# Attention stage of a hybrid block: ScalarE instead of VectorE copies the turned maxima of each half sequence to 16 bits

## The reference

```python
def _L0_attn_b_ref(x, W_qkv, W_q_lsr, W_k_lsr, lsr_core, W_o):   # x: 32 sequences, 256 tokens, 128 wide; 16 heads of 8
    ql = jnp.einsum('bhtd,hdr->bhtr', q, W_q_lsr)
    kl = jnp.einsum('bhsd,hdr->bhsr', k, W_k_lsr)
    scores = jnp.einsum('bhtr,bhsr->bhts', ql * lsr_core[None, :, None, :], kl) * scale
    scores = jnp.where(causal[None, None], scores, -jnp.inf)
    attn = jax.nn.softmax(scores, axis=-1)
    y = jnp.einsum('bhts,bhsd->bhtd', attn, v)
    return y.transpose(0, 2, 1, 3).reshape(b, t, d) @ W_o
```

## Time and profile before

| | us |
|---|---|
| median of 3 runs | 2333.87 (2331.89 to 2334.64) |
| profiled execution, its own time | 2342.5 |
| its span, first to last instruction | 2340.8 |
| granted PE clock over the span | 0.827 of full speed; 1.00 from 1180 to 1740 us |
| DVE busy | 1857.7 (79%) |
| PE busy | 1654.0 (71%) |
| ACT busy | 1471.0 (63%) |
| POOL busy | 1342.9 (57%) |

### The profile page before, as it was taken

The page is one execution under the profiler, slowest core; times in us unless marked ns, Lnnn a source line. Parts: engine busy times, 40 slices in busy tenths (PEclk is TensorE's granted clock), DMA queues, the critical chain, the costliest instruction groups (busy, mean ns, idle before and its releaser), DMA issues. The chain is left out here.

```text
span 2340.8 us, 52167 instructions
## 1 busy us (share of the span) xinstructions
PE 1654.0 (71%) x16780; PEld 1352.2 (58%) x16780; DVE 1857.7 (79%) x4943; ACT 1471.0 (63%) x3849; POOL 1342.9 (57%) x1496
## 2 busy tenths in 40 slices
PE   4676675766657369995689999999986459998000
PEld 2444454454546158884488888888875338887000
DVE  6999999999978957776689999999975867776221
ACT  5666676766743647774388888888883457776000
POOL 3545555555540045554399999999971035553774
PEclk8778787777865679998699999999995579999555
DMA  1000001010034013333122222222214013333232
GB/s 29 14 14 22 20 14 28 14 27 14 19 104 140 1 48 81 81 80 58 39 57 57 57 59 59 59 57 57 57 28 129 23 27 81 81 81 67 74 80 57
DMA packets 188967, 122.59 MB, mean 52 GB/s; under 512 B 24320, under 2 KB 177824, under 8 KB 188704
## 3 DMA queue, kind: packets, MB, share of 16 engines
q1 hardware_dynamic: 154016, 75.18, 11.6%
q0 software_dynamic: 17408, 35.69, 6.9%
q10 hardware_dynamic: 17280, 8.40, 1.2%
HBM read 66.22 MB, written 44.04 MB: 47 GB/s over the span
## 5 line engine op out<-in xcount | busy, mean ns | idle before, releaser
L1044 POOL DMA_INDIRECT ffn_xs<-normed,ffn_tokeni x288 | 273.1, 948 | 460.1 <-DVE posi L1420 260.7
L1877 POOL TENSOR_TENSOR att_pl<-att_p,att_ph 128x384 f16<-128x384 f32 x512 | 455.3, 918 | 56.3 <-ACT att_ph L2098 48.6
L323 POOL TENSOR_TENSOR sq<-states,qS 128x256 f32<-128x256 f32 x256 | 250.9, 980 | 304.3 <-DVE states L733 303.3
L543 ACT ACTIVATE decayed<-states,alpha 128x64 f32<-128x64 f32 x1024 | 272.3, 336 | 177.6 <-DVE states L733 175.7
L379 PE MATMUL bank<-sq,ident 128*128 128x128 f32 x1024 | 249.9, 415 | 93.4 <-POOL sq L323 93.4
L2206 DVE TENSOR_REDUCE att_mx<-bank 128x3 f32<-128x384 f32 x512 | 279.9, 552 | 41.0 <-PE bank L1934 36.8
L1251 ACT ACTIVATE ffn_h<-bank,b_cols 128x256 f32<-128x256 f32 x576 | 226.4, 475 | 127.7 <-PE bank L1139 117.4
L379 PEld LDWEIGHTS bank<-sq,ident 128*128 128x128 f32 x1024 | 220.0, 240 | 128.9 <-POOL sq L323 100.7
L2095 ACT ACTIVATE att_p<-bank 128x384 f32<-128x384 f32 x512 | 252.2, 493 | 58.9 <-PE bank L1971 55.5
L2098 ACT ACTIVATE att_ph<-bank 128x384 f16<-128x384 f32 x512 | 253.0, 494 | 0.0
L1152 PE MATMUL bank<-w_h,ffn_hh 128*128 x1152 | 225.6, 223 | 14.9 <-DVE ffn_hl L1439 4.5
(11 more groups left out here) (336 smaller groups left out, 5085.5 us busy)
## 6 DMA issues: line engine op xcount, KB each, us to landing
slots<-ffn_ys SPq DMA_DIRECT2D x144, 128.0 KB
ffn_x_all<-x SPq DMA_DIRECT2D x16, 512.0 KB, 4.8
normed<-ffn_xn ACTq DMA_DIRECT2D x32, 256.0 KB, 2.3
att_qz<-att_qp SPq DMA_DIRECT2D x256, 32.0 KB
ffn_xs<-normed,ffn_tokeni POOLq DMA_INDIRECT x288
xin<-in_x SPq DMA_DIRECT2D x64, 64.0 KB, 2.0
xres<-in_x SPq DMA_DIRECT2D x64, 64.0 KB, 2.0
x<-x SPq DMA_DIRECT2D x64, 64.0 KB, 1.8
```

The costliest lines, as they stand in the source:

```text
L323: nc.gpsimd.tensor_tensor(sq[:, t, :].rearrange("p (h i j) -> p h i j", h=HL, i=D), states[:, t, :].rearrange("p (h i j) -> p h i j", h=HL ...
L543: ins = nc.scalar.activation(decayed[:, 64 * h:64 * h + 64], states[:, (t - 1) % TC, 64 * h:64 * h + 64], ACT.Copy, scale=alpha[p][:, t, h ...
L1044: pool.indirect_dma_start(xs[j % AHEAD][:, r, :], None, A["normed"], bass.IndirectOffsetOnAxis(ap=tokeni[:, BR * j + r:BR * j + r + 1], ax ...
L1877: nc.gpsimd.tensor_tensor(pl[:, h % RP, :], p32[:, h % RP, :], ph[:, h % RP, :], ALU.subtract).then_inc(low_done, 1)
```

## The change

The copy of the turned maxima to `mst` (L2237) leaves DVE and goes to ACT as an activation with the function Copy, in a new function `maxima_rows`; 64 copies of 128x512 elements move. On ACT it stands behind the exponentials of head 3 (second half) and of head 11 (first half). A new semaphore `maxi_act` counts the copies; SP and PE wait for it where they waited for DVE's count. For the first sequence the copy stands between two small pieces of the layer norm of sequence 2.

```diff
-MAXI_SECOND_AT = dict(larger1=0, high1=0, low1=0, rows1=3)
-MAXI_FIRST_AT = dict(larger0=9, high0=9, low0=9, rows0=11)
+MAXI_SECOND_AT = dict(larger1=0, high1=0, low1=0)
+MAXI_FIRST_AT = dict(larger0=9, high0=9, low0=9)
...
+MAXI_ACT_AT = {3: 1, 11: 0}
...
+        def rows_written(eng, b, n):
+            eng.wait_ge(maxi_act, 2 * b + n + 1)
...
             def place(i, p, n):
                 b = NBUF * i + p
-                sp.wait_ge(maxi_dve, at(MAXI, b, f"rows{n}"))
+                rows_written(sp, b, n)
...
                 elif name == "q23":
                     if not under(b, 2):
-                        pe.wait_ge(maxi_dve, at(MAXI, b - 2, "rows1"))
+                        rows_written(pe, b - 2, 1)
...
+            def maxima_rows(i, p, n):
+                b = NBUF * i + p
+                act.wait_ge(maxi_pe, 2 * b + n + 1)
+                if not under(b, 1):
+                    ii, pp = sooner(i, p, 1)
+                    act.wait_ge(m_in[n][pp], 16 * HL * (ii + 1))
+                a(mst[n][:, :, :].rearrange("p g t -> p (g t)"), ps_x[n][:, :], ACT.Copy).then_inc(maxi_act, 1)
...
-            for name in FRONT_ACT:
+            for name in FRONT_ACT[:-1]:
                 front(name, 0, 2)
+            maxima_rows(0, 0, 0)
+            front(FRONT_ACT[-1], 0, 2)
...
                 for h in range(H):
                     exps(i, p, h)
+                    if h in MAXI_ACT_AT and (MAXI_ACT_AT[h] or later(i, p, 1)):
+                        maxima_rows(*((i, p) if MAXI_ACT_AT[h] else later(i, p, 1)), MAXI_ACT_AT[h])
...
-                else:
-                    dve.wait_ge(maxi_pe, 2 * b + n + 1)
-                    if not under(b, 1):
-                        ii, pp = sooner(i, p, 1)
-                        dve.wait_ge(m_in[n][pp], 16 * HL * (ii + 1))
-                    ins = v.tensor_copy(mst[n][:, :, :].rearrange("p g t -> p (g t)"), ps_x[n][:, :])
```

More of the change, by code:

```diff
@@ L1648 @@
 FRONT_DVE_HELD = [n for n in FRONT_DVE if n not in ("xn0", "xn1", "x_low")] + ["scale", "xn0", "x_low"]
-MAXI = ["maxima0", "larger0", "high0", "rows0", "maxima1", "larger1", "high1", "rows1"]
+MAXI = ["maxima0", "larger0", "high0", "maxima1", "larger1", "high1"]
+MAXI_ACT_AT = {3: 1, 11: 0}
 NBUF = 4
@@ L1700, in attention @@
         (ready, cleared, front_dve, front_act, front_pe, proj_pe, proj_act, proj_dve, maxi_dve, maxi_pe, tail_dve, tail_pe,
-         tail_act, s_ps, max_done, st_ps, exp_done, high_done, low_done, pv_done) = (
+         tail_act, s_ps, max_done, st_ps, exp_done, high_done, low_done, pv_done, maxi_act) = (
             sem(n) for n in ("ready", "cleared", "front_dve", "front_act", "front_pe", "proj_pe", "proj_act", "proj_dve",
                              "maxi_dve", "maxi_pe", "tail_dve", "tail_pe", "tail_act", "s_in_psum", "max_done",
-                             "st_in_psum", "exp_done", "high_done", "low_done", "pv_done"))
+                             "st_in_psum", "exp_done", "high_done", "low_done", "pv_done", "maxi_act"))
         ps_s, ps_st, ps_y, ps_x = bank[0:2], bank[2:4], bank[4:6], bank[6:8]
@@ L1892, in front @@
                 if not under(b, 2):
-                    pe.wait_ge(maxi_dve, at(MAXI, b - 2, "rows0"))
+                    rows_written(pe, b - 2, 0)
                 for k in range(TB):
@@ L1949, in turn_max @@
                 else:
-                    pe.wait_ge(maxi_dve, at(MAXI, b - 1, "rows1"))
+                    rows_written(pe, b - 1, 1)
                 for s in range(2):
@@ L1995, in tail_turn @@
                 elif later(i, p, 1):
-                    pe.wait_ge(maxi_dve, at(MAXI, b + 1, "rows0"))
+                    rows_written(pe, b + 1, 0)
                 else:
@@ L2274, in _ @@
                 for name in MAXI_FIRST_AT:
-                    if MAXI_FIRST_AT[name] == h and name != "rows0":
+                    if MAXI_FIRST_AT[name] == h:
                         maxi(name, 0, 0)
-            maxi("rows0", 0, 0)
             for name in FRONT_DVE:
```

## The result

The changed kernel takes 2342.66 us (median of 9 runs, 2338.26 to 2349.53), the kernel before 2335.14 us beside it (9 runs, 2331.89 to 2343.28): ratio 1.0035, 95% interval 1.0022 to 1.0048. That is 8.2 us slower (5.1 to 11.2). The forecast was 2341.3 us, 7.4 us above before.

A forecast was written before the change was run, and what follows sets the result against it. Waits, not engine shares, were taken to bound the attention step. 29 steps at 0.18 us (5.2) plus 2.2 for the ends made 7.4 us, put on the median 2333.87: 2341.3 us, range 2335 to 2350.

The forecast's parts named there:

- q23 is held by ACT's copy, k01 0.17 late: Behind head 3, the second-half copy ends later on ACT: q23 starts 0.26 us late, k01 and the step 0.17.
- The first half's copy is 0.01 late: Behind head 11, ACT's copy ends at 1381.09 instead of 1381.08, on the path of the place DMAs to `st(0)`.
- The exponentials of heads 12 and 13 move back by up to half a microsecond: On ACT behind the first-half copy; `st(14)` and `st(15)`, two heads later, were to come about when these are ready.
- POOL's lag to ACT grows and shrinks with the step, and costs nothing.: In the steady attention step, POOL running behind ACT's exponentials was to add no time.
- The rival that DVE was the bound, capped by POOL's 0.17 us of slack: Steady step: freeing DVE makes the kernel faster, at most 0.17 us a step, 4.9 us, near 2329.0; chance 0.10.
- The ends, 2.2 us: Outside the steady steps: 0.8 us once before the first step, 1.4 at the end; from nothing to 3.
- The sum: 29 steady steps at 0.18 us give 5.2, plus 2.2 for the ends: 7.4 us slower, 2341.3 us.
- The signs: Trace signs: q23 waits about 0.3 us each step, step 19.35, DVE about 43 us less busy, ACT 38 more.

The follow-up runs named there:

- e1: The changed kernel with only the second half's copy on ACT (head 3), the first half's back on DVE at head 11: step 19.32 us, +1.8 us against before.
- e3: The changed kernel with the second half's copy behind head 2 instead of head 3, the first half's still behind head 11: step 19.13 us, ratio 1.0006.
- e2: The changed kernel with only the first half's copy on ACT (head 11), the second half's back on DVE at head 3: step 19.31 us, +6.1 us against before.
- e8: Only the first half's copy on ACT, and POOL subtracts only half the columns for head 14 in every sequence but the first: step 19.17 us.
- e9: The changed kernel with the second half's copy on ACT behind head 2, the first half's back on DVE at head 11: step 19.00 us, 0.9976 of before.
- e11: The changed kernel with the first half's copy behind head 10 instead of 11 in the last four sequences: 43.2 us after the 29th `att_xout`, ratio 1.0032.
- e12: Both copies on ACT, second half's behind head 2, first half's behind head 11 but head 10 in the last four sequences: ratio 0.9995.
- e4: The changed kernel with both copies one head earlier on ACT, behind heads 2 and 10: most steps 19.13 us, -2.3 us against before.
- e5: The kernel before, unchanged, profiled again for a second trace: step 19.16 us, 44.3 us from the 29th `att_xout` to the last.
- e6: The kernel before with a spare POOL copy of 128x4 integers behind the subtraction of head 14 in each step: step 19.30 us.
- e7: The kernel before with a spare POOL copy of 128x4 integers behind the subtraction of head 7 in each step: step 19.20 us.

## Why the prediction was right, point by point

*q23 is held by ACT's copy, k01 0.17 late.* Right in each link: +0.27 at q23, +0.18 at k01, no wait at `tail_turn` in the steady steps, 19.35 for the step. e1 shows that this copy alone costs 0.15, e3 that it costs nothing at q23 one head earlier.

*The first half's copy is 0.01 late.* This holds only in the company of the other. "The exponentials of heads 12 and 13 move back by up to half a microsecond" was seen, but its way on to POOL, from there to DVE's add and back to q23 was not. Alone it costs 0.14 (e2, e8). In the change POOL and the add are as late as in e2, but q23 waits for ACT's copy anyway. That the step's 0.18 was hit is in part luck: by e1 and e2 one delay hid behind the other, which the prediction had not worked out.

*"POOL's lag to ACT grows and shrinks with the step, and costs nothing."* Wrong as a statement, see above, without harm to the sum.

*The rival that DVE was the bound, capped by POOL's 0.17 us of slack.* It fell for this change. The cap was right: with the second half's copy at head 2 and the first half's left on DVE (e9) the step is 19.00, 0.17 below before, and the kernel 5.4 us faster (3.4 to 7.7). So moving work off DVE can pay; its load alone didn't decide. The Trainium skill's rule on offloading to ScalarE ("Perfetto Trace Analysis", Optimizing Scalar/DVE Operations) says that it may make sense to offload work where VectorE is saturated. It comes true here for one copy at head 2 (0.9976), and not for the two at heads 3 and 11 (1.0035).

*The ends, 2.2 us.* Mis-sized. Before the first step +0.9 was measured (0.8 forecast). After the 29th `att_xout` it was +4.2 instead of 1.4. Of the three distances there, the one with `st(0)` of the thirty-first step grew by 2.6, the others by 1.2 and 0.4. The prediction's sum had nothing for the thirty-first step, and its range for the ends, up to 3 us, had 0.8 for it. It took each link's lateness and left the clock as it was; a longer wait at `st(0)` stood there with a stretch at 1.2 GHz. In e11 and e12, where the wait is short, the clock stayed at 2.4.

*The sum.* The 28 distances up to the 29th `att_xout` at 0.18 are 5.0, with the measured ends 10.1. The profiles give 7.0 between the first add and the last `att_xout` (0.9 + 6.1), because before had one step of 21.57 us in its own trace; against its second trace (80.86 and 583.07 us for the two stretches) it is 9.4. The timed runs give 8.2 (5.1 to 11.2). The forecast of 7.4 lies in that interval, though its ends were less than half of the 5.1 measured, so that the number came out this near is in part luck; the base of 2333.87 was 1.3 below the median of the nine runs.

*The signs.* The wait at q23 was 0.20 us where about 0.3 was named. DVE is 30.8 us less busy over the kernel and ACT 23.7 more, where 43 and 38 were named; these were the full durations of 64 copies, which overlap in part with the rows around them (the copy above by 0.11 and 0.12).

## What to carry to other kernels

Before an operation is moved to a less busy engine, look at which instruction it must stand behind there and who waits for the result: with both copies on ACT, one head earlier for the second half turned 0.18 us a step lost into 0.04 won (e3), and with the first half's copy left where it was, into 0.17 won (e9). Then follow what the moved operation pushes back on its new engine through every reader, also an engine that "only" runs alongside: POOL had 0.15 us of room and handed the rest on. Delays of two edits need not add up in a step, so a sum that is right for both together says little about either alone.

## What the runs showed of the hardware

- A float32 add on VectorE with both inputs in SBUF did not finish while GpSimd's subtraction ran: the first pair of adds of a step ended 0.40 to 0.44 us after it in all fourteen profiles, whatever its own start (0.62 us busy in e8, 0.94 in before and 1.18 in e2 for the same work).
- The 128x512 copy from PSUM to 16 bits took 0.60 us on ScalarE and 0.68 on VectorE (medians of 64). Behind an activation of 0.48 us it started 0.37 after that one's start, 0.11 before its last write.
- TensorE waited 2.0 us at `st(0)` of the thirty-first step in two kernels and its granted clock fell to 1.2 GHz: in the change 1.1 us behind the end of the wait, for 3.4 us, in e3 0.6 us before its end, for 6.8. In the other profiles the wait there was 1.35 us or less and the clock stayed at 2.4. The length of a wait doesn't decide alone: 2.3 us between two matmuls in another step of e4 went by without a fall, and behind the same 1.64 us in the same program it fell in one execution (e5) and not in the other.
- A spare 128x4 integer copy on GpSimd was recorded as 0.18 to 0.19 us and pushed the next instruction back by 0.15 (e6, e7).
- One step now and then is much longer: 25 to 26 us in e7, e8 and e9, 21.6 in before. In e7, e8 and e9 alike DVE had waited 2.0 to 2.1 us for gathered rows, its two adds then took 3.6 to 3.7 us beside POOL's subtractions, and TensorE's granted clock fell to 1.2 GHz behind that. What made those rows late isn't known. It blurs comparisons of single profiles.
